# Setting the last batch's steps up to six slots later in a transformer layer's slot plan

## The reference

```python
x = x + attention(layernorm(x))     # 16 heads, causal, then a 128x128 product and a bias
n = layernorm(x)
shared = (silu(n @ Wg.T) * (n @ Wu.T)) @ Wd.T
probs = sigmoid(n @ router.T + bias)              # 8 experts
scores, idx = top_k(probs, 2); scores /= sum(scores)
routed = sum over the two of scores * ((silu(n @ gate_w[e]) * (n @ up_w[e])) @ down_w[e])
return x + shared + routed
```

## Time and profile before

| | |
|---|---|
| median of 3 runs | 705.58 us (703.97 to 706.2) |
| profiled execution, its own time | 704.36 us |
| its span | 702.6 us |
| PE busy | 638.1 us, 91% |
| DVE busy | 538.8 us, 77% |
| ACT busy | 456.4 us, 65% |
| POOL busy | 307.8 us, 44% |
| mean granted clock | 0.975 |

### The profile page before, as it was taken

One profiled execution on the slowest core, in us unless ns is written; L12 is line 12 of the kernel. 1 busy time (PEld: TensorE's weight loads), 2 busy tenths in 40 slices (PEclk: granted clock), 3 DMA queues, 4 the chain that ended last, 5 costly groups with the idle time before them and its releaser, 6 DMA issues.

```text
span 702.6 us, 16427 instructions
## 1 busy us (share of the span) xinstructions
PE 638.1 (91%) x5432; PEld 402.7 (57%) x5432; DVE 538.8 (77%) x1903; ACT 456.4 (65%) x816; POOL 307.8 (44%) x511
## 2 busy tenths in 40 slices
PE   7489999999999999998999999999986788898983
PEld 7255555555555555554455555555565577786653
DVE  5799877798788878799878877878257745576886
ACT  3367776767767768776677866776745545565651
POOL 4393631323133223223478422422664276546673
PEclk9699999999999999999999999999999999999996
DMA  9200543621121112211241110211553376794424
GB/s 253 68 1 3 158 133 110 176 86 47 51 77 46 35 33 84 55 56 39 58 133 65 54 52 17 57 38 41 118 119 107 83 133 129 146 176 91 113 58 131
DMA packets 102768, 60.24 MB, mean 86 GB/s; under 512 B 44568, under 2 KB 94640, under 8 KB 102688
## 3 DMA queue, kind: packets, MB, share of 16 engines
q1 hardware_dynamic: 66144, 28.22, 16.7%
q10 hardware_dynamic: 32336, 22.29, 11.1%
q0 software_dynamic: 4208, 8.69, 4.8%
HBM read 19.62 MB, written 30.77 MB: 72 GB/s over the span
## 4 chain that ended last, share of the span: by engine, by line
PE 73%; DVE 11%; issue 5%; ACT 4%; another core or an unknown queue 1%; POOL 1%; ACTq 0%; DVEq 0%; POOLq 0%
PE bank L1058 9%; PE bank L1037 9%; PE bank L1075 9%; PE bank L1060 8%; PE bank L1059 8%; PE bank L998 4%; PE bank L1166 4%; PE bank L1000 4%; PE bank L999 4%; PE bank L1164 3%; PE bank L1165 3%; DVE junk L1455 2%; PE bank L1202 2%; PE bank L1204 2%; PE bank L1203 2%
## 5 line engine op out<-in xcount | busy, mean ns | idle before, releaser
L1327 ACT ACTIVATE p_sb<-bank,inv_scale 128x512 f32<-128x512 f32 (+1 forms) x384 | 222.1, 614 | 43.2 <-PE bank L1060 35.0
L1455 DVE CUSTOM_DVE_ANT_0 junk<-bank,causal 128x512 bf16<-128x512 f32 (+3 forms) x512 | 222.0, 483 | 29.0 <-PE bank L1037 27.5
L931 POOL TENSOR_SCALAR_AFFINE_SELECT p_sb<-p_sb 128x384 f32<-128x384 f32 x128 | 66.8, 522 | 280.3 <-ACT p_sb L1327 279.4
L1059 PE MATMUL bank<-ql,ah 128*128 128x512 f16 (+3 forms) x512 | 153.1, 299 | 0.0
L1060 PE MATMUL bank<-qh,al 128*128 128x512 f16 (+3 forms) x512 | 152.7, 299 | 0.0
L1058 PE MATMUL bank<-qh,ah 128*128 128x512 f16 (+3 forms) x512 | 146.9, 300 | 0.3 <-ACT p_sb L1327 0.3
L1037 PE MATMUL bank<-ah,qh 128*128 128x512 f16 (+3 forms) x512 | 130.1, 300 | 1.2 <-DVE low L1455 1.2
L1427 DVE TENSOR_TENSOR ql<-bank,qh 128x512 f16<-128x512 f32 x128 | 88.3, 690 | 42.8 <-ACT qh L1292 40.5
L1292 ACT ACTIVATE qh<-bank 128x512 f16<-128x512 f32 x128 | 76.4, 597 | 34.4 <-PE bank L1000 33.0
L1639 DVE SCALAR_TENSOR_TENSOR al<-bank,gu_scale,ah 128x512 f32<-128x512 f32 x69 | 51.6, 748 | 59.5 <-ACT ah L1358 43.1
L978 POOL DMA_INDIRECT p_sb<-ys_dram,place x64 | 67.9, 1061 | 39.6 <-PE bank L1166 17.4
(11 more groups left out here) (246 smaller groups left out, 1127.0 us busy)
## 6 DMA issues: line engine op xcount, KB each, us to landing
o_dram<-oT ACTq DMA_DIRECT2D x32, 256.0 KB, 2.3
ys_dram<-ql ACTq DMA_DIRECT2D x25, 256.0 KB
xs_dram<-causal ACTq DMA_DIRECT2D x6, 832.0 KB, 4.5
wst<-in_Wkqv SPq DMA_DIRECT2D x8, 264.0 KB, 5.0
x_sb<-in_x SPq DMA_DIRECT2D x8, 256.0 KB, 6.1
out<-x_sb SPq DMA_DIRECT2D x8, 256.0 KB
o_all<-o_dram SPq DMA_DIRECT2D x7, 256.0 KB
r_all<-r_dram SPq DMA_DIRECT2D x7, 256.0 KB
```

The source lines that it names most:

```text
L1059: nc.tensor.matmul(bank, m.ah[:, keys], ql[:, s, c * P:N], start=False, stop=False)
L1327: nc.scalar.activation(p_sb[v % P_RING][:, S_AT[k]:S_AT[k] + S_WIDTH[k]], m.psum[S_BANK[k]][:, 0:S_WIDTH[k]], ACT.Exp, scale=m.inv_scale[: ...
L1455: last = nc.vector.tensor_tensor_reduce(out=junk[:, S_AT[k] + at:S_AT[k] + at + w], in0=m.psum[M_BANK[k]][:, at:at + w], in1=m.causal[:, N ...
```

## The change

The slots of the last batch's steps from spread on are set later, by one slot (spread, proj) to four (late, late_copy, logits, exp) and three (split). Statistics, aggregates and the three root steps, which were in two slots, now stand in four. The third part's steps move by five (sort, count, rank), six (place, expert, send) and nine (weigh). No instruction is added or taken away.

```diff
-LAST_STEPS = {"gather": 1, "rinv": 2, "spread": 3, "mult": NEVER, "proj": 4, "stats": 4, "aggr": 4, "newton0": 5, "newton1": 5, "newton2": 5, "norm": 5, "late": 6, "late_copy": 7, "logits": 8, "exp": 9, "split": 10}
+LAST_STEPS = {"gather": 1, "rinv": 2, "spread": 4, "mult": NEVER, "proj": 5, "stats": 6, "aggr": 7, "newton0": 8, "newton1": 8, "newton2": 9, "norm": 9, "late": 10, "late_copy": 11, "logits": 12, "exp": 13, "split": 13}
-LAST_PART_STEPS = {"sort": 9, "weigh": 10, "count": 11, "rank": 12, "place": 12, "expert": 13, "send": 13}
+LAST_PART_STEPS = {"sort": 14, "weigh": 19, "count": 16, "rank": 17, "place": 18, "expert": 19, "send": 19}
```

## The result

| | kernel before | changed kernel |
|---|---|---|
| median of 16 runs each, same chip | 706.00 us (703.15 to 710.74) | 711.36 us (708.85 to 714.71) |
| ratio, 95% interval | | 1.0074 (1.0053 to 1.0095) |
| profiled execution's span | 702.6 us | 711.3 us |

The median lies 0.4 us above the range that was given (702.0 to 711.0), and slower by more than 0.3% where no difference was forecast.

A forecast was written before the change was run, and what follows sets the result against it. TensorE was taken to bound the kernel, with a dip after attention and a tail held by GpSimd's fetches. Tail +6.8 and dip -6.0 gave +0.8 us: 705.2 us profiled, 706.4 against the median, range 702.0 to 711.0.

The forecast's parts named there:

- The slots of sends and fetches: Expert stage: third part's sends move to slots 160 to 170, first fetch to 171, last to 213; twelve fetches behind unit 67.
- The price at the end: Tail: six more fetches behind unit 67, then landing and last adds, cost 6.8 us (5.8 to 8.7).
- the lower of the two terms: Tail: six added fetches at 1.25 us each with DVE idle, 7.5 us; the other term was 8.7, and 7.9 was taken.
- DVE has four of the earlier tiles to add in that time too: Tail: DVE adds earlier tiles during the six added fetches, so 7.9 us was taken between 7.5 and 8.7.
- the gap before the last eight adds: Tail, a sign: DVE would show a gap before its last eight adds; without one the forecast is wrong.
- The named waits of the dip: After attention, PE's waits for `hn`, `picked`, the output bank and `r_all`: 10.1 us now, 2.1 + 0.4 + 1.4 + 2.9 after.
- I take +1.0 for both together: gain 6.0: Dip: +1.0 us for returning send stops and newly open PE stops together, making the gain 6.0 us, ends 3 and 10.
- the clock's term of the walk: Dip: lower clock behind the `hn` and `picked` waits costs 3.4 us now; only 1.7 us, behind `picked`, would stay.
- the crowd of stops at units 17 to 22: Units 17 to 22: 4.7 us excess from the first third-part send; returns six slots later or is gone, 0 to 4.7.
- stops that stand open: Dip: PE's stops without a releasing engine, hidden behind named waits, come into the open where those go; 0 to 2 us.
- the walk's 5.0 us: Dip, slot by slot: 13.5 us lost to waits and clock now, 8.5 after, a gain of 5.0 us.
- The third one: Rival, slots 145 to 160: PE's own stops fill freed waits, fetches cost in full; +3.8 to +5.7 us, chance 0.28.

The follow-up runs named there:

- kernel b: The kernel before with only its fetches moved to the changed kernel's slots (171 to 213); 715.03 us, ratio 1.0085.
- e: The kernel before without its 64 fetches (routed experts' part of the output missing); 690.58 us, ratio 0.9777.
- g: The changed kernel without its 64 fetches (expert part of every output row wrong); ratio to the kernel before 0.9789.
- kernel d: The kernel before without the third part's 16 sends (that part's expert rows wrong); 702.98 us, ratio 0.9908.
- i: The changed kernel without its last ten fetches, slots 207 on (outputs partly wrong); 704.29 us, ratio to the kernel before 0.9945.
- m: The changed kernel without the second part's 24 sends (its expert rows wrong); 706.33 us, ratio to the kernel before 0.9967.
- kernel f: The kernel before with each indexed fetch replaced by a plain transfer of 128 consecutive rows, same size and queue; ratio 0.9783.
- kernel k: The changed kernel with the first part's 24 fetches two to a slot (171 to 182), the rest at their old slots; 713.25 us, ratio 1.0065.

## Why the prediction was wrong, step by step

**The slots of sends and fetches** were right: first fetch behind unit 32, twelve behind unit 67, stream's end 15.0 us behind its SiLU ("some 16"). (Of the steps themselves, weigh moved by nine slots and not by the title's six.)

**The price at the end** was right in kind and 1.0 us short: 6.8 forecast, 7.8 measured in the change and 8.0 in kernel b. The six more fetches lengthened the stream by 6.6 us (15.0 against 8.4), less than the 7.9 taken: eleven of the twelve take 0.94 to 0.96 us and follow each other at 1.25 us. So the lower of the two terms was the better one, but not because DVE was idle: it works until 692.98, beside the first half of the twelve. The rule of the Trainium skill on DVE and GpSimd ("SBUF — State Buffer", section "SBUF: two separate sides") speaks of only some of DVE's operations, and in this trace only one kind lengthens a fetch by more than 0.2 us. Every fetch of the changed kernel over 1.1 us (up to 1.48) starts 0.02 to 0.35 us after L1642 has started, an operation that takes 0.68 us, and none of the last twelve does. (Behind L1610 a fetch takes up to 1.06 us.) What was short is the work behind the stream: landing and eight adds were put at 4.15 us, and 7.5 us pass from the stream's end to the end of the adds, since a shared product's addition and all sixteen adds wait for it (5.3 before; from there to the end it is 2.8 now and was 3.7, so 6.6 + 2.2 - 0.9 = 7.9). The step "DVE has four of the earlier tiles to add in that time too" missed that DVE's order puts L1634 ahead of them, and that it waits. The forecast had the gap before the last eight adds; it came before 21 of them.

**The named waits of the dip** were right for `hn` (2.2, forecast 2.1), `picked` (2.4, forecast 2.9) and `r_all` (none). That the output bank's 2.4 us lie near the forecast of 1.4 is luck: the 1.4 us were to stand behind the exponentials in slot 154, but PE waits for the bank at 530.4 and 536.6 us, in the slots of units 8 and 10, at boundaries that were put at nothing. Behind the exponentials stands the 2.2 us stop in its place.

**What failed is the step "I take +1.0 for both together: gain 6.0"**, and with it the clock's term of the walk. Of its two things the crowd of stops at units 17 to 22 was listed as worth 0 to 4.7 us; it came back with the sends (6.0 us between units 22 and 33, kernels e and g), so it was worth nothing. The other, stops that stand open, was put at 0 to 2 us as a loss; one stop of 2.2 us before unit 16 appeared in every trace with the new part steps. And the loss of clock that was to go stayed (two falls up to unit 17, as before), so that nothing of its 1.7 us was gained. Of the walk's 5.0 us that leaves 3.3 us of named waits against 2.2 us of a new stop: about 1 us, as kernel d against the changed kernel says at unit 22. Behind unit 33 the changed kernel's trace loses the clock twice more (3.4 us). Kernels g, i and m, with the same steps, have no falls there, so these two may belong to the execution and not to the change; that stays open. The whole gain is 0 by the two traces, 1 to 2 us by kernel d, 1.9 by the traces of e and g, and 2.4 us by the medians with the tail. By ratios it can't be told from nothing: kernel b, the late stream alone, 1.0085 against the change's 1.0074, and kernels e and g 0.9777 against 0.9789.

**The range** was also put together from two starting points: its lower end is 705.58 - 3.6, its upper 706.4 + 4.6. From 705.58 the upper end would have been 710.2, and the miss 1.2 us. Unit 22's SiLU came at 573.54 us, just outside the 567 to 573 that were named.

**The rivals.** The third one is nearest: the late fetches cost in full and the dip gives back little. It was given +3.8 to +5.7 us, and 5.4 was measured. Its mechanism, PE's own stops in the freed waits, holds for the one stop before unit 16; the rest of what was lost came with the sends. It had a chance of 0.28 against 0.38. The row that should have moved it up was already in hand: the fetches' pace at units 32 to 39 of 0.5 us a slot above the 1.98 us of matmuls. It was read as PE's own habit. Taken as the price of the indexed transfer in each slot it says that sends moved to a later slot take their price along.

**What stays open.** What makes the stop before unit 16, PE's register reads or something else. What of an indexed transfer stops PE, its index handling on POOL or its scattered rows: kernel f changed both at once. Two rows to one issue, which would halve the number of issues, was not tried. Nor was the new `LAST_STEPS` without the new part table: its exponentials stand in slot 13 of the batch's steps, behind the sort of the old table in slot 9. And whether it is PE or DVE that is held in the 8.3 us of the tail: PE's records of its last products end at 696.7 us, DVE goes on at 701.25.

No version beat the kernel before with all its work done. The experiments point to fewer indexed issues, not to other slots for them.

## What to carry to other kernels

When steps are moved to later slots, follow what a planner hangs on them to the last slot of the program: here the diff names no fetch, and six fetches more behind the last gate cost as much as the whole change (kernel b). Look for the engine's waits without a releaser elsewhere in the trace, ask which transfers they go with, and count them at the new place. Compare waits and clock over the same work and not over the same stretch of time, and over the whole program: here a gain of 7 us in the middle was for the most part sends that had not been paid for yet. When such stops follow a transfer, move or remove that transfer by itself before you build on the gap around it.

## What the runs showed of the hardware

Indexed transfers issued by GpSimd slow TensorE, though they write a buffer (`p_sb`) that its products of that stage don't read: the 58 fetches up to unit 67 cost 14.7 us of PE's progress, and as many plain transfers of the same bytes from the same engine and queue cost nothing (kernel f, 163.6 against 163.7 us at unit 67 with no transfers at all). The price grows with density: at two to a slot (kernel k, units 33 to 44) a unit takes 3.3 us, at three to two slots 2.2 us (the kernel before, same units) to 2.7 us (the change), with none 2.0 us (kernels e, f and g).

An indexed fetch takes 0.94 us of GpSimd, and up to 1.48 us when it starts just after DVE's subtraction L1642 (0.68 us); beside DVE's other operations of that stage it stays under 1.1 us.

TensorE's granted clock falls to the lower level in pieces that cost the same 1.7 us each, three to eight between units 0 and 67 of one execution, and executions of kernels with the same steps differ in their number.

In the tail, where PE has next to nothing left, an addition on DVE that needs no fetched row came 8 us late as long as indexed fetches were being issued (the change and kernel b), and at once when they were not (kernel i).
